# The inflow product of a Mamba scan waits for a nearer unit and moves to the end of its unit on GpSimd

## The reference, cut to what matters

```python
dA  = jnp.exp(jnp.einsum('bld,dn->bldn', delta, A))
dBu = jnp.einsum('bld,bln,bld->bldn', delta, Bm, xc)
def step(h, inp):
    dA_t, dBu_t, C_t = inp
    h = dA_t * h + dBu_t
    y = jnp.einsum('bdn,bn->bd', h, C_t)
    return (h, y)
```

## Time and profile before

| | |
|---|---|
| median of 3 runs | 844.0 us (843.27 to 844.61) |
| the profiled execution, its own time | 846.1 us |
| its span in the profile | 844.3 us |
| VectorE busy | 739.2 us, 88% of the span |
| TensorE busy | 649.8 us, 77% |
| GpSimd busy | 581.2 us, 69% |
| ScalarE busy | 506.5 us, 60% |
| mean granted TensorE clock | 0.889 of full speed |

### The profile page before, as it was taken

One profiled execution on the slowest core, in us unless ns is written; L12 is line 12 of the kernel. 1 busy time (PEld: TensorE's weight loads), 2 busy tenths in 40 slices (PEclk: granted clock), 3 DMA queues, 4 the chain that ended last, 5 costly groups with the idle time before them and its releaser, 6 DMA issues.

```text
span 844.3 us, 12617 instructions
## 1 busy us (share of the span) xinstructions
PE 649.8 (77%) x3545; PEld 465.3 (55%) x3545; DVE 739.2 (88%) x1145; ACT 506.5 (60%) x1091; POOL 581.2 (69%) x487
## 2 busy tenths in 40 slices
PE   4438688878778877887877876886876789888991
PEld 2124445545355536764566635873554457788990
DVE  1376998989999999999999999999999897686774
ACT  2545795876688577464846577555854775444440
POOL 1094675677977797689958896789846994456451
PEclk9659899989989898997989988897887899999995
DMA  6923233223323336542464336532424621123247
GB/s 175 263 104 103 87 113 113 82 84 97 116 69 107 106 102 182 158 145 99 130 174 140 109 96 203 148 110 94 133 91 128 171 61 33 39 65 83 65 129 231
DMA packets 80248, 99.94 MB, mean 118 GB/s; under 512 B 10215, under 2 KB 48051, under 8 KB 80163
## 3 DMA queue, kind: packets, MB, share of 16 engines
q1 hardware_dynamic: 75859, 90.21, 36.3%
q0 software_dynamic: 4320, 8.92, 3.0%
HBM read 87.56 MB, written 15.35 MB: 122 GB/s over the span
## 4 chain that ended last, share of the span: by engine, by line
DVE 37%; PE 34%; issue 17%; ACT 7%; DMA 2%; POOL 2%; DVEq 1%; SPq 0%; ACTq 0%; POOLq 0%
DVE state L1077 18%; PE work_front L1248 4%; PE y L1288 4%; DVE product L1087 4%; PE up L1399 2%; PE work_front L1254 2%; PE y L1284 2%; PE up L1410 2%; PE gate L1392 2%; DVE stats L1007 2%; ACT decay L941 1%; DVE silu_m L1213 1%; PE gate L1313 1%; DVE arena L1052 1%; PE work_side L1332 1%
## 5 line engine op out<-in xcount | busy, mean ns | idle before, releaser
L818 POOL TENSOR_TENSOR inflow<-du,b_wide 128x1024 f32<-128x1024 f32 x128 | 315.5, 2468 | 145.0 <-DVE product L1087 92.0
L1077 DVE TENSOR_TENSOR_SCAN state<-decay,carry,inflow 128x512 f32<-128x512 f32 x192 | 234.7, 1264 | 6.5 <-ACT decay L941 6.5
L1087 DVE TENSOR_TENSOR product<-state,c_wide 128x1024 f32<-128x1024 f32 (+1 forms) x93 | 139.1, 1495 | 4.4 <-PE y L1284 3.3
L941 ACT ACTIVATE decay<-arena,a_neg 128x512 f32<-128x512 f32 x128 | 86.6, 688 | 60.7 <-DVE state L1077 56.9
L1284 PE MATMUL y<-ident,product 128*128 128x128 f32 x664 | 106.4, 305 | 20.6 <-DVE product L1087 20.5
L1284 PEld LDWEIGHTS y<-ident,product 128*128 128x128 f32 x664 | 87.2, 158 | 62.5 <-issue 34.7
L848 POOL DMA_INDIRECT y_dram<-y_rows,x_rows x71 | 82.5, 1162 | 56.0 <-ACT y_rows L997 49.1
L941 ACT ACTIVATE decay<-delta_odd,a_neg 128x512 f32<-128x512 f32 x128 | 86.6, 689 | 56.3 <-DVE state L1077 56.1
L1288 PE MATMUL y<-h_rows,ident 128*128 128x512 f32 x180 | 100.9, 652 | 7.0 <-ACT h_rows L906 6.5
L842 POOL DMA_INDIRECT row_dram<-m_tok,place x64 | 74.4, 1163 | 24.3 <-issue 12.7
L1077 DVE TENSOR_TENSOR_SCAN state<-decay,inflow 128x512 f32<-128x512 f32 x64 | 74.5, 1203 | 6.1 <-ACT decay L941 3.6
(11 more groups left out here) (232 smaller groups left out, 1342.6 us busy)
## 6 DMA issues: line engine op xcount, KB each, us to landing
b_wide<-bc_dram SPq DMA_DIRECT2D x128, 256.0 KB, 3.3
c_wide<-bc_dram SPq DMA_DIRECT2D x93, 256.0 KB, 3.5
w_stage<-gate_up_dram SPq DMA_DIRECT2D x26, 344.0 KB, 4.2
x_rows<-row_dram SPq DMA_DIRECT2D x71, 65.0 KB, 1.9
arena<-gate_up_dram SPq DMA_DIRECT2D x8, 344.0 KB, 4.4
x_tok<-in_x SPq DMA_DIRECT2D x8, 256.0 KB, 5.8
out<-x_tok SPq DMA_DIRECT2D x8, 256.0 KB, 4.8
inflow<-y_dram SPq DMA_DIRECT2D x6, 256.0 KB, 4.4
```

Of the source, the lines that this page charges most:

```text
L818: e.tensor_tensor(inflow[:, key % 3], du[:, c % 2], b_wide[:, key % ROW_SLOTS:key % ROW_SLOTS + 1, :].to_broadcast([P, HALVES, CHUNK]), AL ...
L941: e.activation(decay_bank[h][:], delta[c % 2][:, h, :], ACT.Exp, scale=a_neg[:, h, n:n + 1]).then_inc(S["decay"], 1)
L1077: e.tensor_tensor_scan(state[:, key % STATE_SLOTS, h, :], decay_bank[h][:], inflow[:, key % 3, h, :], 0.0 if c % (SEQ // CHUNK) == 0 else ...
L1087: e.tensor_tensor(product[:, key % 2, :, :wide], state[:, key % STATE_SLOTS, :, :wide], c_wide[:, key % ROW_SLOTS:key % ROW_SLOTS + 1, :wi ...
```

## The change

The inflow of unit i + 2 is put last among the steps of unit i, and it waits for the product of unit i (or, without one, its scans) in place of that of unit i - 1. Nothing else is edited; no operation is added or left out.

```diff
@@ plan()
         back = take_back(1)
         fetch("fetch_b", i + 4)
         fetch("fetch_c", i + 2)
-        fetch("inflow", i + 2)
         if i:
             put("total0", i - 1)
...
             free.append(i)
         put("times_c", i)
+        fetch("inflow", i + 2)
     for r in range(2):
         put(f"total{r}", len(UNITS) - 1)
@@ GpSimd
                     e.wait_ge(S["du"], c + 1)
-                    if key >= 3:
-                        if share[key - 3] < SUB:
-                            e.wait_ge(S["times_c"], products[key - 3])
+                    if key >= 2:
+                        if share[key - 2] < SUB:
+                            e.wait_ge(S["times_c"], products[key - 2])
                         else:
-                            e.wait_ge(S["scan"], HALVES * (key - 2))
+                            e.wait_ge(S["scan"], HALVES * (key - 1))
                     e.tensor_tensor(inflow[:, key % 3], du[:, c % 2], b_wide[:, key % ROW_SLOTS:key % ROW_SLOTS + 1, :].to_broadcast([P, HALVES, CHUNK]),
                                     ALU.mult).then_inc(S["inflow"], 1)
```

## The result

The changed kernel takes 861.5 us (median of 4 runs, 858.3 to 863.5) against 844.3 us (median of 4, 843.3 to 846.2): ratio 1.0192, 95% interval 1.0165 to 1.022. It is slower, by 17.2 us between the medians. The two profiled executions differ by less, 860.9 to 846.1 us, in spans 858.8 to 844.3, so 14.5 us; the rest lies between runs and is not explained by a trace. In later series the kernel before had medians of 845.5 to 846.6 over 13 to 23 runs, so a part of the 17.2 may be that its first 4 runs were low in its own spread.

What follows compares the result with a forecast made beforehand. The prediction took VectorE to be the bound, so later scans delay everything. Net stalls in chunks 3 to 7 summed to 13.5 us, giving a median of 857.5 us, 1.6% slower, in the range 850.5 to 864.

Steps and rivals of the forecast that it cites:

- Stalls in full: Rival: collisions counted as vanished come back elsewhere, so no stall is recovered; 864 us, band 861 to 865, chance 0.10.
- the five clusters: Units behind list steps and x_sum in chunks 3 to 7, where late inflows stall scans; net 2.5 to 3.1 us each.
- The order on GpSimd: Each gap between units keeps one inflow waiting for the same product; phase unchanged, only the reserve falls by one unit.
- ten waits: VectorE waits for inflows before scans of units 56, 57, 72, 73, 88, 89, 104, 105, 125, 126; longest about 2.4 us.
- in either order: Chunk 5: product of unit 88 and inflow of gap 88 both end at 508.2 us, whichever goes first; scans 3.8 us late.
- net 2.7 us: Chunk 4: scans 4.7 us late, less 2.0 us back from a front step no longer held by three inflows in a row.
- 3.1 us late: Chunk 7: last scans' delay from late inflows of gaps 124 and 125, with the copy into w_stage losing nothing.
- The tail: After the last scans: its chain starts at them, so chunk 7's 3.1 us passes on in full and its length stays.
- The sum: Five cluster terms, 2.6 + 2.7 + 2.5 + 2.6 + 3.1 = 13.5 us, giving a median of 857.5 us.
- SyncE's queue: Later fetch_b and the loads behind it cost nothing, with over 8 us of cover for B and over 4 for C.
- Faster: Rival: nearer wait frees held products if stalls stay under 1.3 us; gains up to 5.9 us, 838 us, chance 0.05.
- the handover: Between product and inflow on the shared port: costs nothing; the skill page would add about 0.9 us, giving 858.4 us.

Runs made afterwards that it cites:

- one_further: Changed kernel's place and waited event, but putting the inflow of unit i + 3 there instead of i + 2; 848.1 us beside 845.7 for the kernel before, ratio 1.0008.
- old_in_list_units: Changed kernel with old place and wait in states 0 to 9 of chunks 3 to 6 and all of chunk 7; 859.7 us, ratio 1.0171.
- each half of the edit: Kernel before with the nearer wait alone, 884.5 us, ratio 1.0451; with the inflow last in its unit but the old wait, 885.1 us, ratio 1.0466.
- after_copy_early: Changed kernel with the first early copy into w_stage moved from state 13 to state 11 of chunk 7; 858.7 us, ratio 1.0155.
- new_in_chunk7: Kernel before with the change in chunk 7 alone; 849.1 us, ratio 1.0045.
- the three tries at the kernel before: Kernel before with x_sum one row later, 845.3 us; an empty row ahead of list2, 846.6 us; x_sum behind rstd2 in state 4's unit, 849.5 us.

## Why the prediction held, and where not

*The number.* The forecast was 857.5 us, and the median is 861.5. That is inside the range of 850.5 to 864, but 0.5 us above the forecast's own band (854 to 861) and so, by the number, in the band of "Stalls in full". By the mechanism it is the forecast: stalls at the five clusters, of which a part comes back.

*The order on GpSimd.* Held: the phase stayed, scans outside the clusters kept their distance, and one_further shows the same order in another writing at no cost behind the head. What was taken is one unit of reserve; with it given back in the units behind the list steps (old_in_list_units), the waits behind them are gone. How much the phase is worth I had not asked: each half of the edit shifts it, and costs nearly 40 us.

*The clusters.* All five stalled, in the units named, and no others waited for an inflow. I had said ten waits and there are seven. Ahead of the scans of units 89 and 105 the inflow went before the product, and ahead of those of unit 126 before the copy, so the stall lies in the duration of these. The first stall of each cluster came at its size (2.3, 2.3, 1.3, 2.0, 2.0 us). In chunk 5 the series of list steps, product and inflow gave 3.5 us (512.53 - 504.38 = 8.15, less the 4.67 us by which the chunk already ran later) for 3.8, and 1.4 came back for 1.3. Chunk 6 did the same (3.5 us, 1.4 back, net 2.1 for 2.6); chunk 3 had 3.8. The difference is who goes first, which I took to be of no account ("in either order"). With the product first (chunk 3, from 317.82 to the scans at 321.45) the series lasts 3.6 us. With the inflow first (chunk 5) it lasts 3.4 from the inflow's start at 509.17 and 3.3 from 509.24, when the product was ready. Net, the clusters of chunks 5 and 6 cost 0.4 to 0.5 us less each than forecast.

*Chunk 4.* The term "net 2.7 us" was mis-sized: 1.7. The second stall is 4.5 us for 4.9, and the held operation at L1052 gives back 1.7 for 2.0, since the step ahead of it got longer; these two nearly cancel. The rest is a gain that I had not counted. The short `shift` step of unit 75, which a late inflow held for 1.08 us before, takes 0.13, and with it 1.0 us comes back.

*Chunk 7.* The term "3.1 us late" was mis-sized: 4.9. I had the copy go ahead of the inflow of gap 125 and lose nothing. It came 0.16 us too late and was held for 2.1 us, with a further 0.8 for the subtraction behind gap 126's. The list steps had come through faster: from the inflow of gap 124 to that of gap 125 it is 4.6 us (699.91 to 704.52) where it was 5.0. A further 0.5 us was lost between the scans of units 118 and 124, which no term covers and no run explains. after_copy_early takes 2.6 us away, new_in_chunk7 shows the loss without the other clusters. I read from the earlier trace rows that this copy can be held, and then took the outcome of a race as given.

*The tail* passed the shift on: from the last scans to the end of the span 145.5 us, before 145.0. The mean granted TensorE clock was lower (0.872 against 0.889), and yet the tail is only 0.5 us longer.

*The sum.* 13.5 forecast; 13.9 measured at the last scans, of which 0.45 were there ahead of the first cluster; 14.5 in the spans. That it fits so well is luck: chunks 4 to 6 came 1.8 us lower than forecast in sum, and chunk 7 came 1.8 us higher. The medians are 3 us further apart than the profiled pair. What makes that is open; no run was spent on it, and a part may be the low first series of the kernel before.

*SyncE's queue* cost nothing that the trace shows: no product waited for its row of C and no inflow for its row of B. The cover was thinner than I wrote, though: three units of 3.7 us less 3.3 leave under 8 us, and a unit without a product lasts 2.4 us, so that the shortest three leave 3.9 us for a row of B.

*The rivals.* "Stalls in full" lies nearer to the median than it deserves: its mechanism, collisions that come back, was seen in chunk 7 alone. "Faster" fails at its own condition: the first stalls are 1.3 to 2.3 us. Products at units 57 and 105 do take 1.2 us, as that rival had it.

On the handover, the Trainium skill's page "SBUF — State Buffer", section "A bandwidth-pool intuition that's wrong (but worth ruling out)", would add some 115 ns each time. The changed kernel's trace doesn't show it: the inflow at 502.05 lasted 3.40 us with a product that ended at 503.24, which leaves 2.21 us of the inflow's 2.35.

## What to carry to other kernels

When a step is moved in an in-order queue and its wait is moved with it, write the queue out as gaps between the other steps, before and after: here the sequence of waits turned out the same, and only the index had slipped, so a reserve of two units had become one. Then the first stall of each place can be priced from the trace of before alone: the end of each producer is held against the start of the consumer one earlier. What follows the first stall is harder, and it is where terms were off by 1.0 and 1.8 us. The places to look at are those behind bursts on the producer's engine.

Where two engines hold each other up, as VectorE's steps with operands in SBUF and GpSimd's inflows do here, a producer that runs beside an operation that is not held (here a scan) is free. Elsewhere it costs up to its whole length (2.35 us here), even to steps of 4 columns. So an edit that shifts such an engine against the other can cost more than a stall (39 us for each half of this edit), and in the three tries at the kernel before a gain at one collision was paid at the next.

## What the runs showed of the hardware that was not expected

- A VectorE step of 4 columns with two operands in SBUF takes 0.13 us alone (431.36, changed kernel), 1.08 us behind the rest of an inflow of GpSimd (425.79, kernel before) and 2.64 us through a whole one (578.95, kernel before, with an inflow from 579.21 to 581.56); the 128 x 688 copy takes 0.48 or 2.57 us. Scans between them, whose decay lies in PSUM, stay at 2.31 to 2.46 us a pair.
- Which of the two goes first was settled by 0.07 us in chunk 5 of the changed kernel (509.17 and 509.24), and the same engine order gives 1.2 us for the product of unit 56 and 3.4 for that of unit 88. The two together take 3.4 or 3.6 us, so the race is seen mostly in the durations and little in the total, unless another step stands between.
- An indirect DMA on GpSimd is stretched by a product as well. In the kernel before, one issued beside the product of unit 65 (369.20 to 370.42) takes 1.91 us, its neighbour behind it 0.95:

```profile
369.39 1.91 POOL L848 DMA_INDIRECT y_dram<-y_rows,x_rows  x1 [0.17 <-issue]
371.61 0.95 POOL L842 DMA_INDIRECT row_dram<-m_tok,place  x1 [0.31 <-issue]
```
